# Attention maxima copied from SBUF to SBUF by six transfers instead of through DRAM, turned one slot later, with the next query projected one slot later

## What is computed

```python
x = x + tanh(g_xattn[0]) * wkv(layernorm(x), ctx)                 # layer 1
x = x + tanh(g_ffn[0])   * gated_ffn(layernorm(x))                # layer 2
x = x + tanh(g_xattn[1]) * attention(layernorm(x), ctx, mask)     # layer 3
x = x + tanh(g_ffn[1])   * moe_ffn(layernorm(x))                  # layer 4

q = einsum('oc,bct->bot', Wq, target) + bq     # k, v alike from ctx
dot = einsum('bhdt,bhds->bhts', q, k) / sqrt(8)
mask = target_mask[:, :, :, None] * source_mask[:, :, None, :]
dot = mask * dot - (1.0 - mask) * 1e6
amap = softmax(dot, axis=-1) * mask
out = einsum('bhts,bhds->bhdt', amap, v)
```

## Time and profile before

| | us |
|---|---|
| median of 3 executions | 559.36 (553.83 to 560.2) |
| the profiled execution | 558.33, its span 556.5 |
| mean granted TensorE clock in it | 0.972 |
| PE busy in the span | 483.7 (87%) |
| DVE busy | 379.6 (68%) |
| ACT busy | 247.5 (44%) |
| POOL busy | 229.2 (41%) |

### The profile page before, as it was taken

How to read it: one execution, slowest core, us unless ns; L and a number is a source line. 1 busy time by engine, 2 the same in 40 slices (tenths; PEclk the granted TensorE clock), 3 DMA queues, 4 the chain that set the end, 5 groups by cost and what they waited for, 6 DMA issues and landing times. The chain is left out here.

```text
span 556.5 us, 10469 instructions
## 1 busy us (share of the span) xinstructions
PE 483.7 (87%) x3384; PEld 264.7 (48%) x3384; DVE 379.6 (68%) x768; ACT 247.5 (44%) x478; POOL 229.2 (41%) x303
## 2 busy tenths in 40 slices
PE   2859999998898788988898989787979989899994
PEld 2634564745533433333333433332434545688873
DVE  4986879788589777788788888795757433333331
ACT  2732233121232177878788888677711100133321
POOL 2753224142367165666555565412110730024424
PEclk9987999999999979999999999899999999999998
DMA  7747600000175525555556665510050241168753
GB/s 214 214 145 166 104 1 0 1 1 2 57 195 143 130 57 150 147 143 143 141 141 147 162 156 135 146 28 5 1 157 1 91 165 47 58 167 185 196 127 38
DMA packets 67254, 59.94 MB, mean 108 GB/s; under 512 B 10048, under 2 KB 62256, under 8 KB 67216
## 3 DMA queue, kind: packets, MB, share of 16 engines
q1 hardware_dynamic: 63424, 55.24, 36.9%
q0 software_dynamic: 3072, 4.21, 4.4%
q10 hardware_dynamic: 720, 0.00, 0.1%
HBM read 38.90 MB, written 22.50 MB: 110 GB/s over the span
## 5 line engine op out<-in xcount | busy, mean ns | idle before, releaser
L1175 DVE TENSOR_REDUCE MX<-psum 128x2 f32<-128x512 f32 x256 | 161.3, 683 | 34.4 <-PE psum L1054 33.4
L1215 ACT ACTIVATE HP<-psum 128x512 f32<-128x512 f32 x256 | 137.5, 598 | 56.4 <-PE psum L1068 55.4
L1054 PE MATMUL psum<-QKA 60*128 60x256 bf16 x512 | 83.7, 281 | 13.8 <-DVE MX L1175 10.1
L1068 PE MATMUL psum<-QKA 60*128 60x256 bf16 x512 | 79.4, 281 | 16.1 <-DMA QKA<-max_scr 12.6
L1141 PE MATMUL psum<-HP,VP 128*32 128x256 f32 x1024 | 84.0, 402 | 0.2 <-ACT HP L1215 0.2
L512 PE MATMUL psum<-space_a,space_w 128*128 128x512 f32 x160 | 75.0, 618 | 1.1 <-ACT space_a L497 0.8
L1054 PEld LDWEIGHTS psum<-QKA 60*128 60x128 bf16 x512 | 35.9, 96 | 69.3 <-DVE MX L1175 47.9
L1736 POOL DMA_INDIRECT out_x<-OE,to_u x16 | 25.0, 1564 | 75.7 <-ACT OE L1777 73.2
L512 PEld LDWEIGHTS psum<-space_a,space_w 128*128 128x128 f32 x160 | 30.3, 197 | 37.9 <-issue 35.3
L525 ACT ACTIVATE space_a<-psum,hgs 128x512 f32<-128x512 f32 (+1 forms) x24 | 15.6, 651 | 70.3 <-PE psum L512 47.8
L1875 PE MATMUL psum<-XT,WE 128*128 128x256 f32 (+1 forms) x192 | 44.3, 380 | 2.4 <-ACT XT L1761 1.6
(11 more groups left out here) (186 smaller groups left out, 735.3 us busy)
## 6 DMA issues: line engine op xcount, KB each, us to landing
QKA<-stack_scr SPq DMA_DIRECT2D x32, 480.0 KB, 5.4
stack_scr<-PARTS SPq DMA_DIRECT2D x32, 192.0 KB, 2.0
WE<-in_W SPq DMA_DIRECT2D x16, 352.0 KB
stack_scr<-PARTS SPq DMA_DIRECT2D x32, 128.0 KB, 1.9
XD<-dispatched SPq DMA_DIRECT2D x8, 258.0 KB, 3.7
X<-in_x SPq DMA_DIRECT2D x4, 512.0 KB, 5.6
CTX<-in_ctx SPq DMA_DIRECT2D x4, 512.0 KB, 8.2
MB<-in_mask SPq DMA_DIRECT2D x16, 128.0 KB, 5.7
```

The source lines that it names most:

```text
L1054: return pe.matmul(to[:, tt * T:(tt + 1) * T], QKA[rows, k, 0, h, tt * P:(tt + 1) * P], QKA[rows, k, 1, h, :], start=True, stop=True)
L1068: return pe.matmul(to[:, (m % 2) * T:(m % 2 + 1) * T], QKA[rows, k, 1, h, st * P:(st + 1) * P], QKA[rows, k, 0, h, :], start=True, stop=True)
L1175: dve.tensor_reduce(MX[:, par, head_of(n), :], src[:, :].rearrange("p (a s) -> p a s", a=2), axis=AX.X, op=ALU.max).then_inc(a_red, 1)
L1215: act.activation(PT[:, i % 2, st, 2 * half:2 * half + 2, :].rearrange("p j t -> p (j t)"), TBK3[THIRDS[m]], ACT.Exp).then_inc(a_exp, 1)
```

## The change

It has four parts. (1) `max_scr` is gone. The three parts of the maxima go straight from `NP` to the last rows of `QKA`, by six transfers of one destination partition each (two halves of the heads by three parts); `a_mx` counts 96 per batch instead of 32. `pool_np` waits for the preceding six before it overwrites `NP`. (2) SP's order per batch is now: mask row of b + 5, the six of the maxima of b + 1, the fill of b + 3, the store of b + 4. (3) The maxima are turned inside slot 1, ahead of its scores, and ACT copies them behind the exponentials of slot 1; the query of b + 5 is projected at the end of slot 7 and ACT reads it behind the exponentials of slot 0 of the next batch. (4) Ahead of the slots, query projections 2, 3 and 4 are issued at other places, the wait for all of layer 2's result is split over the first two PSUM banks, and the last group's layer norm statistics (four `bn_stats`, then the rest) are spread over slots of the first three batches.

The diff shows, in this order, SP's functions, ACT's slots, PE's slots (the turning, then the projection), and DVE's work ahead of the slots and in them.

```diff
-                def sp_max_store(sp, g, k):
-                    b = GB * g + k
-
-
-                    sp.wait_ge(a_np, b + 1)
-                    alone(sp)
-                    sp.dma_start(max_scr[k % 2].rearrange("r p c -> p r c"), NP[:, :, :]).then_inc(a_mscr, 16)
-
                 def sp_max_fill(sp, g, k):
-                    sp.wait_ge(a_mscr, 16 * (GB * g + k + 1))
+                    sp.wait_ge(a_np, GB * g + k + 1)
                     alone(sp)
                     for half in range(2):
-                        lo = 64 * half + STACK - 3
-                        sp.dma_start(QKA[lo:lo + 3, k, 0, :, :],
-                                     max_scr[k % 2, :, HEADS * half:HEADS * (half + 1), :].rearrange("r (h t) c -> r h (t c)", t=2))\
-                          .then_inc(a_mx[k], 16)
+                        for r in range(3):
+                            lo = 64 * half + STACK - 3 + r
+                            sp.dma_start(QKA[lo:lo + 1, k, 0, :, :].rearrange("o h (t c) -> o (h t) c", c=P),
+                                         NP[HEADS * half:HEADS * (half + 1), r, :]).then_inc(a_mx[k], 16)
...
                         def sp_batch(g, k):
                             b = GB * g + k
-                            if there(b, 3):
-                                sp_fill(sp, *at(g, k, 3))
-                            if there(b, 1):
-                                sp_max_store(sp, *at(g, k, 1))
                             if there(b, 5):
                                 sp.wait_ge(a_masked, b + 2)
                                 alone(sp)
                                 sp_mask(sp, *at(g, k, 5))
                             if there(b, 1):
                                 sp_max_fill(sp, *at(g, k, 1))
+                            if there(b, 3):
+                                sp_fill(sp, *at(g, k, 3))
                             if there(b, 4):
                                 sp_store(sp, *at(g, k, 4))
...
-                            if p == 0 and there(b, 1):
+                            if p == 0 and not first(b) and there(b, AHEAD_Q):
+                                act_qk(act, b + AHEAD_Q)
+                            if p == 1 and there(b, 1):
                                 act_nm(act, b + 1)
-                            if p == 7 and there(b, AHEAD_Z):
-                                act_qk(act, b + AHEAD_Z)
...
+                            if p == 1 and there(b, 1):
+                                if there(b, AHEAD_Q):
+                                    pe.wait_ge(a_qk, b + AHEAD_Q + 1)
+                                else:
+                                    pe.wait_ge(a_x3, b - 1)
+                                pe_mxT(pe, *at(g, k, 1))
                             if there(b, AHEAD_S):
                                 pe_both(pe, at(g, k, AHEAD_S), (g, k), p)
...
-                            if p == 0 and there(b, 1):
-                                if there(b, AHEAD_Q):
-                                    pe.wait_ge(a_qk, b + AHEAD_Q + (0 if first(b) else 1))
-                                else:
-                                    pe.wait_ge(a_x3, b - 1)
-                                pe_mxT(pe, *at(g, k, 1))
...
+                            if p == 7 and there(b, AHEAD_Z):
+                                if first(b):
+                                    pe.wait_ge(a_nm, 2)
+                                else:
+                                    pe.wait_ge(a_x3, b)
+                                pe_proj_q(pe, *at(g, k, AHEAD_Z))
...
+                        dve_z3(dve, AHEAD_Q)
                         reduces(1, 0, 16)
                         dve_x2(dve, G3, DB)
-                        dve_stats3(dve, ln3, G3)
...
+                            if isinstance(b, int) and 8 * b + p in LAST_STATS:
+                                dve_one_of_last(dve, ln3, LAST_STATS.index(8 * b + p))
```

More of the change, by code:

```diff
@@ L54, in flamingo_kernel @@
     mask_scr = nc.dram_tensor("mask_scr", [9, B, T], bf16).ap()
-    max_scr = nc.dram_tensor("max_scr", [2, 3, 2 * HEADS, P], bf16).ap()
     dispatched = nc.dram_tensor("dispatched", [SLOTS, ROW], fp32).ap()
@@ L211, in flamingo_kernel @@
             NS = GB
+            G3 = NG - 1
             HALF = HEADS // 2
@@ L662, in dve_stats3, with dve_one_of_last @@
                    .then_inc(a_var, 1)
+            def dve_one_of_last(dve, ch, i):
+                if i < GB:
+                    ch.do(dve.bn_stats(stats3[:, i, :], X[:, GB * G3 + i, :]))
+                    return
+                ch.wait()
+                alone(dve)
+                for t in range(GB):
+                    ch.do(dve.bn_aggr(mv3[:, GB * G3 + t, :], stats3[:, t, :]))
+                ch.wait()
+                dve.tensor_scalar(veps3[:, GB * G3:B], mv3[:, GB * G3:B, 1], EPS, None, ALU.add).then_inc(a_var, 1)
             def pool_power3(pool, g):
@@ L1119, in pe_both @@
                         to = SBK3[THIRDS[n]]
+                        if first(GB * to_turn[0] + to_turn[1]) and p == 0:
+                            pe.wait_ge(s_x2, 1 + 2 * G3 + n + 1)
                         score_bank(pe, *to_score, n)
@@ L1161, in pool_z3 @@
                 def pool_z3(pool, pch, b):
-                    pool.wait_ge(a_rstd, NG)
+                    pool.wait_ge(a_rstd, b // GB + 1 if isinstance(b, int) else NG)
                     pool.wait_ge(a_proj, b)
@@ L1241, in pool_vp, with pool_np @@
                     last.then_inc(a_vp, 1)
-                def pool_np(pool, pch, b):
+                def pool_np(pool, pch, b, sent=None):
                     pool.wait_ge(a_nm, b + 1)
-                    if later(b):
-                        pool.wait_ge(a_mscr, 16 * b)
+                    if sent:
+                        pool.wait_ge(a_mx[sent[1]], 96 * (sent[0] + 1))
                     nil = zeros[0:2 * HEADS, 0:P]
@@ L1329, in flamingo_kernel @@
                 LN4, TURN4 = 3, 9
+                LAST_STATS = [2, 4, 10, 12, 18]
                 with nc.Block() as block:
@@ L1394, in slot @@
                                 act_exp(act, g, k, p // 2, p % 2)
-                            if p == 0 and there(b, 1):
+                            if p == 0 and not first(b) and there(b, AHEAD_Q):
+                                act_qk(act, b + AHEAD_Q)
+                            if p == 1 and there(b, 1):
                                 act_nm(act, b + 1)
-                            if p == 2 and first(b):
-                                act_qk(act, AHEAD_Q)
-                            if p == 7 and there(b, AHEAD_Z):
-                                act_qk(act, b + AHEAD_Z)
                             if p in (3, 5) and there(b, AHEAD_Q):
@@ L1434, in slot @@
                                 pool_power4(pool, tail(b, p) - LN4)
-                            if p == 0 and not first(b) and there(b, AHEAD_Q):
+                            if p == 0 and there(b, AHEAD_Q):
                                 pool_masked(pool, *at(g, k, AHEAD_Q))
                             if p == 1 and there(b, 1):
-                                pool_np(pool, pch, b + 1)
-                            if p == 2 and first(b):
-                                pool_masked(pool, *at(g, k, AHEAD_Q))
+                                pool_np(pool, pch, b + 1, (g, k))
+                            if p == 3 and isinstance(b, int) and b == 2:
+                                pool_power3(pool, G3)
                             if p == 4 and there(b, AHEAD_Z):
@@ L1493, in slot @@
                                 pe_pv(pe, *at(g, k, -1), 3, st)
-                            if p == 0 and there(b, 1):
-                                if there(b, AHEAD_Q):
-                                    pe.wait_ge(a_qk, b + AHEAD_Q + (0 if first(b) else 1))
-                                else:
-                                    pe.wait_ge(a_x3, b - 1)
-                                pe_mxT(pe, *at(g, k, 1))
-                            if p == 1 and first(b):
-                                pe.wait_ge(a_nm, 2)
-                                pe_proj_q(pe, *at(g, k, AHEAD_Q))
-                            if p == 6 and there(b, AHEAD_Z):
-                                if first(b):
-                                    pe.wait_ge(a_qk, AHEAD_Z)
-                                else:
-                                    pe.wait_ge(a_x3, b)
-                                pe_proj_q(pe, *at(g, k, AHEAD_Z))
                             if p == 3 and there(b, -1):
@@ L1554, in slot @@
                                 dve_reduce(dve, *at(g, k, AHEAD_S), 2 * p)
-                            if p == 1 and first(b):
-                                dve_z3(dve, AHEAD_Q)
                             if there(b, AHEAD_S):
                                 dve_reduce(dve, *at(g, k, AHEAD_S), 2 * p + 1)
+                            if isinstance(b, int) and 8 * b + p in LAST_STATS:
```

(1 more changed line is left out.)

22 lines of the change are left out of this document (10 added, 12 removed).

## The result

The changed kernel takes 621.63 us (median of four, 620.54 to 622.76) against 559.09 us: the ratio is 1.114, with a 95% interval of 1.107 to 1.121. It is slower, as forecast, but by 62.5 us and not by 19, and outside the range of 558 to 590. The mechanism that was forecast is what the trace shows; two of its terms were far too small, one of them by 2 us in every batch.

A forecast was written before the change was run, and what follows sets the result against it. It took batches of 13.3 us, with PE waiting for maxima queued behind the stack's fill, as the bound. From 558.3, 12 x (15.2 - 13.3) = +22.8 and -2.9 for smaller savings gave 578 us, range 558 to 590.

The forecast's parts named there:

- Which wait takes the place of the one removed: At each batch start, PE would wait 2 to 3 us for the stack's fill instead of 12.6 us in all for maxima.
- The six issues: On SP, the six transfers of the maxima would take 0.29 us each to issue, 1.75 for all, ahead of the fill.
- The upper bound of 0.41: On SP, the range's slow end: six issues at 0.41 us each, adding 0.7 us to a batch, toward 590 us.
- its bounds of 1.5 and 5.8: The six transfers' landing: after 1.5 us at t = 9.6, or after 5.8 at t = 13.9, both hidden before 15.2.
- The clock: PE at half clock after idling: about 0.2 us if it falls at slot 1; 0.1 us a batch counted as mean.
- the chain up to the copy: From PE's first score through slots 0 and 1 to ACT's copy of the maxima: 3.9 us.
- The fill: The stack's fill on SP, from its issue to PE's start of the next batch: 6.7 us taken.
- The rivals with a quicker fill: Stack's fill of 4.5 us, total 551 to 555 us, chance 0.08; or about 5.3, total 560 us, chance 0.06.
- the estimate of 4.3 us: The stack's fill by the skill's rule, 2.0 us plus bytes over 436 GB/s: period 12.8, total about 549 us.
- Ahead of the slots: Before the hardware loop: split bank waits and moved projections save 1.2 us; the first batch takes 13.9, saving 1.3.
- The rival that ended faster: In each batch the fill is in time and a batch takes 12.2 us: 542 us in total, chance 0.07.
- The rival of maxima landing late: The six transfers take 5.8 us each in a row, ending after t = 16: period 17 or more, 600 us, chance 0.05.

The follow-up runs named there:

- the exchange on SP alone: The changed kernel with SP issuing the stack's fill of b + 3 ahead of everything that waits for the maxima: 546.76 us, ratio 0.980 to the kernel before.
- 541.7 us: The kernel before with the maxima's store to DRAM ahead of the stack's fill, plus the changed kernel's edits ahead of the slots: 541.72 us, ratio 0.969.

## Why the prediction was wrong in size and right in kind

**Which wait takes the place of the one removed: right.** The fill behind the maxima, waited for by the first instruction of each of 12 batches, is what the trace shows, and the exchange on SP alone takes 75 us away. The sign was forecast from it. What failed are the prices of the terms in the loop, below.

**The six issues: mis-sized.** The step "two of the fills of the maxima take 0.58, so 0.29 each and 1.75 for six" took the price of an issue from a transfer of another form: DRAM to three partitions, in place of 16 SBUF partitions to one. The row of all the six issues in the changed kernel (ns min/median/max), and the line below it:

```profile
L1294 SPq DMA_DIRECT2D QKA<-NP x96: 503/589/1182, 179.8 to 453.2; - x96
...
DMA to landing us min/median/max: 1.6/1.7/3.5
```

0.59 each; from the first of six to the fill 4.1 us (364.83 to 368.96, and in the mean of twelve) instead of 2.1. That is 2.0 us in each of 12 periods, 24 us, the largest part of the miss. The upper bound of 0.41 was too low as well, and a row at hand spoke against it: the six stores of a stack, which come from SBUF too, hold SP for 3.23 us, where six times 0.41 is 2.5. The landing, on which the text spent its bounds of 1.5 and 5.8, is 1.7 us and hidden, as said.

**The clock: named, and mis-sized.** The step "matmuls between the turning and the fourth exponential take twice their time, about 0.2 us" took the case, in which the clock fell only after the start of the batch. The text calls it the one stall of that kind, which it was not: in the kernel before PE also waited 1.91 us up to 220.73 and 2.02 us up to 274.63, and the mean clock was 0.69 from 220 to 224 and 0.57 from 276 to 280. With PE idle 3.7 to 5.2 us the clock falls before the start, as the prediction's next sentence has it ("every batch would start its slots slow"), but the sum took only a tenth for it. The copy comes at +4.9 instead of +3.9, and with PE kept busy at +3.75, so that the chain up to the copy was nearly right for the full clock. That is 1.0 us a period, where 0.1 had been counted: 11 us. The two errors feed each other: two issues instead of six, 2.6 us less, gave back 3.2.

**The fill: nearly right.** 6.7 was taken; it took 6.7 to 7.5, 7.1 in the mean of twelve. 0.4 us a period, 5 us. The rivals with a quicker fill fall, and with them the estimate of 4.3 us that the prediction made from the Trainium skill, "DMA: Bandwidth & Descriptors". That section, "Anatomy of one DMA", gives its rule for transfers on the path of GpSimd, and these go out on SP's queue.

Summed, against the forecast of 15.2 with its 0.1 for the clock: 2.0 + 0.9 + 0.4 = 3.3 us and a tenth of rounding, the 18.6 measured; that is 41 us over 12 periods.

**Ahead of the slots: mis-sized, and a small part.** The first slot began at 191.90, where 1.2 us less than 191.62 was forecast. The first batch took 16.05 us (191.90 to 207.95) instead of 13.9, since it runs through the same loop: its six issues began at +5.0 (196.87), as forecast, but the fill at +8.8 instead of +7.2, and it took 7.3 and not 6.7. Together that is 3.6 us: 578 + 41 + 4 = 623, and the profiled execution took 622. In the kernels with the fill first, where this loss is absent, the same edits brought the copy of batch 2's maxima forward by 5.2 us in one pair of runs and by 3.2 in another; why the pairs differ was not looked into.

**The rival that ended faster** (the fill in time, 542 us) was not this kernel, but its point of decision, a fill not behind the maxima, is what 546.8 and 541.7 us came from. The rival of maxima landing late falls with the landing of 1.7 us.

## What to carry to other kernels

Before moving a wait on an in-order queue, follow what is queued behind it until it comes back to the wait: if it does, the terms form a loop and each counts in full in every round, where an error of 2 us is no detail. Of two commands, the large one whose operands are ready goes ahead of the small one that must still wait, and the small one goes ahead as soon as it can be ready in time, as the store of 24 KB that landed in 1.5 us and not in about 6 behind 960 KB of stack (559 to 547 us here). A wait of a few microseconds on PE costs more than itself when it lets the clock fall (1.2 us more here), and the issue of a transfer has to be priced by a transfer of the same form.

## What was not expected of the hardware

An issue on SP of 16 rows of 256 bytes from SBUF to one SBUF partition takes 0.59 us (96 of them), twice that of 12 KB from DRAM to three partitions, 0.29; six small transfers so hold the queue for 3.7 us, while each lands 1.7 us after its issue. After 3.7 to 5.2 us of idleness of PE the granted clock was 0.50 at the restart of all twelve batches, and it was back at 1.00 only 3.0 to 5.7 us into the work. The fill of two times 480 KB let PE start 6.7 to 7.5 us after its issue, 7.1 in the mean with six small transfers ahead of it and 7.0 with two; the one case of before was 6.85. The six small transfers land 1.7 us after their issue when they go out ahead of the fill, and 3.3 or 4.3 us (the medians of two kernels) when they go out behind it.
